# Pacing two gathers per pair of tiles, and moving early row additions, in a mixture-of-experts and attention kernel

## The reference

```python
x = x + 0.5 * ffn(layernorm(x))
x = x + attention(layernorm(x))
x = x + 0.5 * ffn(layernorm(x))      # the same weights

def ffn(x):                                  # 2048 tokens
    scores = softmax(x @ gate.T)             # 32 experts in 8 groups, the best 3 groups count
    weight, index = top_k(masked scores, 6)  # weights are normalised to sum 1
    y = sum over experts e of combine[:, e] * ((silu(x @ w1[e].T) * (x @ w3[e].T)) @ w2[e].T)
    shared = (silu(x @ sw1.T) * (x @ sw3.T)) @ sw2.T
    return y + shared

def attention(x):                            # 16 heads of 16, linear attention with decay
    q, k, v = silu(x @ Wq), silu(x @ Wk), x @ Wv, q and k rotated by position
    o = causal sum with decay in chunks of 128 tokens, with a carried state
    o = rmsnorm per head of o * sigmoid(x @ Wg1 @ Wg2), times a weight
    return o @ Wo
```

## Time and profile before

| | us |
|---|---|
| median of 3 runs | 966.11 (962.2 to 973.23) |
| profiled execution | 960.5 |
| its span | 958.7 |
| PE busy | 772.8 |
| DVE busy | 513.0 |
| POOL busy | 465.3 |
| ACT busy | 358.5 |

### The profile page before, as it was taken

One profiled execution on the slowest core, in us unless ns is written; L12 is line 12 of the kernel. 1 busy time (PEld: TensorE's weight loads), 2 busy tenths in 40 slices (PEclk: granted clock), 3 DMA queues, 4 the chain that ended last, 5 costly groups with the idle time before them and its releaser, 6 DMA issues. The chain is left out here.

```text
span 958.7 us, 16120 instructions
## 1 busy us (share of the span) xinstructions
PE 772.8 (81%) x4554; PEld 609.0 (64%) x4555; DVE 513.0 (54%) x1439; ACT 358.5 (37%) x799; POOL 465.3 (49%) x487
## 2 busy tenths in 40 slices
PE   6895997999969789788889575686999995867486
PEld 6464885888847546576677374564888884645154
DVE  5774942434313537888887469672444431135274
ACT  3160443444424314465665224233444442322000
POOL 3005665553053335867754320655555406456884
PEclk9979898999988898999999755688999998887798
DMA  6862465643233463222220140233444413334524
GB/s 209 338 286 77 158 214 176 231 164 120 89 121 114 159 227 89 80 76 67 72 62 2 34 176 1 77 121 120 153 158 154 138 77 121 126 112 131 207 82 153
DMA packets 42358, 126.43 MB, mean 132 GB/s; under 512 B 8352, under 2 KB 16704, under 8 KB 39488
## 3 DMA queue, kind: packets, MB, share of 16 engines
q1 hardware_dynamic: 23872, 75.40, 20.7%
q0 software_dynamic: 18432, 50.36, 18.0%
HBM read 76.44 MB, written 49.28 MB: 131 GB/s over the span
## 5 line engine op out<-in xcount | busy, mean ns | idle before, releaser
L399 POOL DMA_INDIRECT back<-token_table,slots x192 | 186.7, 973 | 221.9 <-DVE slots L644 96.3
L911 PE MATMUL bank<-w,xt 128*128 x1024 | 260.7, 400 | 33.2 <-ACT xt L492 18.4
L911 PEld LDWEIGHTS bank<-w,xt 128*128 128x128 f32 x1024 | 196.5, 200 | 69.4 <-issue 44.2
L420 POOL DMA_INDIRECT back<-slot_table,combine x124 | 130.0, 1049 | 143.6 <-SPq L328 42.2
L690 DVE TENSOR_TENSOR mids<-mids,bank 128x256 f32<-128x256 f32 x128 | 53.8, 420 | 256.6 <-ACT mids L469 197.3
L931 PE MATMUL bank<-w,mids 128*128 x512 | 142.9, 405 | 4.5 <-DVE mids L697 2.6
L492 ACT COPY xt<-ring 128x256 f32 x256 | 91.5, 408 | 104.0 <-issue 75.9
L931 PEld LDWEIGHTS bank<-w,mids 128*128 128x128 f32 x512 | 93.2, 203 | 16.0 <-issue 7.1
L469 ACT ACTIVATE mids<-bank 128x256 f32<-128x256 f32 x128 | 49.0, 383 | 145.2 <-PE bank L911 87.8
L680 DVE COPY ring<-bank 128x512 f32 (+1 forms) x96 | 66.1, 689 | 46.6 <-PE bank L901 31.2
L923 PE MATMUL bank<-const,mids 128*128 128x128 f32 x256 | 52.6, 290 | 45.7 <-DVE mids L690 24.2
(11 more groups left out here) (209 smaller groups left out, 1070.9 us busy)
## 6 DMA issues: line engine op xcount, KB each, us to landing
slot_table<-gT SPq DMA_DIRECT2D x32, 512.0 KB
slot_table<-ey SPq DMA_DIRECT2D x32, 512.0 KB
w<-in_w SPq DMA_DIRECT2D x12, 1024.0 KB, 17.1
slot_table<-w SPq DMA_DIRECT2D x6, 1024.0 KB
token_table<-back SPq DMA_DIRECT2D x8, 512.0 KB, 2.9
back<-token_table,slots POOLq DMA_INDIRECT x192
x<-in_x SPq DMA_DIRECT2D x4, 512.0 KB, 5.7
turn_a<-in_turn SPq DMA_DIRECT2D x4, 512.0 KB
```

Of the source, the lines that this page charges most:

```text
L399: pool.indirect_dma_start(out=rows[q % RX][:, a * H:(a + 1) * H], out_offset=None, in_=table, in_offset=bass.IndirectOffsetOnAxis(ap=slots ...
L420: pool.indirect_dma_start(out=returned[g % len(returned)], out_offset=None, in_=y_table, in_offset=bass.IndirectOffsetOnAxis(ap=combine[:, ...
L911: last = nc.tensor.matmul(bH[u % 2][:, a * 2 * I:(a + 1) * 2 * I], xt[u % 2][:, a * H + k * P:a * H + (k + 1) * P], w13[:, bass.ds(expert[ ...
```

## The change

It has four parts. (1) Table gathers keep a lead of 4 pairs throughout, in both blocks, and row gathers are let go two per pair from pair 48 (first block) or 47 (second block) on. (2) Rows that come back get more buffers: the space of the first 6 experts in w13 and w2, 18 row buffers, used once these experts' pairs are done; the weights are loaded again at the end of attention. The first column of the first block is added after the last pair, the second in attention as a fifth row; the first two columns of the second block are added after the last pair. (3) In the second block the shared expert's tokens are loaded back in four pieces ahead of SP's last four stores, into free space of the ring. (4) `s_again` becomes four semaphores.

```diff
+GONE = 6
+ADDS = REST + EARLY - 1
+PACED = NQ - NT, NQ - NT - 1
@@
+        spared = [part[:, i * H:(i + 1) * H] for part, n in ((w13, GONE * WE // H), (w2, GONE)) for i in range(n)]
+        s_early = [sem(f"s_early{n}") for n in range(EARLY)]
@@ (first block, then second)
-                    returned = [part[:, i * H:(i + 1) * H] for part, n in ((back, NT), (s1, KS * TB // H))
-                                for i in range(n)]
+                    returned = [back[:, i * H:(i + 1) * H] for i in range(NT)] + spared
...
-                    s1, gTs = w13[:, 0:KS * TB], [w13[:, (u + 1) * KS * TB:(u + 2) * KS * TB] for u in range(2)]
-                    again = w13[:, 3 * KS * TB:3 * KS * TB + KC * T]
-                    returned = [back[:, i * H:(i + 1) * H] for i in range(KEEP)]
+                    products = GONE * WE
+                    s1, *gTs = [w13[:, products + n * KS * TB:products + (n + 1) * KS * TB] for n in range(3)]
+                    spare = (NB % RR + 1) * P
+                    again = [ring[:, a:a + KC * TB] for a in (spare, spare + KC * TB, SPAN + spare, 0)]
+                    returned = [back[:, i * H:(i + 1) * H] for i in range(KEEP)] + spared
@@ (SP)
-                        turns = NQ // 2 // RY - (f == 0)
+                        turns = NQ // 2 // RY - 2
...
+                        sp.wait_ge(e_h, done + NQ - EDGE)
                         if f == 0:
-                            sp.wait_ge(e_h, NQ - EDGE)
                             sp.dma_start(area[:, 0:KC * len(LATE) * TB], columns_table[:, 0:KC * len(LATE) * TB]
                                          ).then_inc(s_here, 16)
+                        else:
+                            stored = columns_table.rearrange("p (k i t) -> p i k t", k=KC, t=TB)
+                            for it in range(T // TB):
+                                sp.dma_start(again[it].rearrange("p (k t) -> p k t", k=KC), stored[:, it]).then_inc(s_again[it], 16)
+                        for it in range(turns, turns + 2):
                             for u in range(RY):
-                                store(turns, u)
+                                store(it, u)
...
                         if f == 1:
-                            sp.wait_ge(e_h, done + NQ)
-                            sp.dma_start(again, columns_table).then_inc(s_again, 16)
@@ (POOL)
-                            if f == 0 and AHEAD <= q < EDGE + RX + AHEAD:
-                                pool.wait_ge(e_xp, q - AHEAD - max(0, q - EDGE - AHEAD) // EDGE + 1)
-                            elif AHEAD <= q < EDGE + AHEAD:
+                            if q >= AHEAD:
                                 pool.wait_ge(e_xp, read + q - AHEAD + 1)
-                            elif q >= RX:
-                                pool.wait_ge(e_xp, read + q - RX + 1)
...
+                                if g == (KEEP if f else NT):
+                                    pool.wait_ge(e_h, done + GONE * NT // 2)
+                                    pool.wait_ge(e_yp, done + GONE * NT // 2)
                                 if g >= len(returned):
                                     pool.wait_ge(s_add, g - len(returned) + 1)
-                                if f == 0 and g % 2 == 0:
-                                    pool.wait_ge(e_h, NQ - NT - 3 + g // 2)
+                                if g % 2 == 0 and PACED[f] + g // 2 <= NQ:
+                                    pool.wait_ge(e_h, done + PACED[f] + g // 2)
@@ (DVE)
-                                if final:
-                                    for g in range(i * 2 * NT // n, (i + 1) * 2 * NT // n):
-                                        add_row(g // NT, g % NT)
...
-                        with dve.Fori(0, (NQ - EDGE - NP) // 2) as it:
+                        with dve.Fori(0, (NQ - NP) // 2 - 1) as it:
                             pairs(it * 2 + NP, 2)
-                        pairs(NQ - EDGE, EDGE, final=True)
+                        pairs(NQ - 2, 2)
                         copy_mid(NQ - 1, NQ - 1)
-                        if f == 1:
...
+                        if f == 0:
+                            for i in range(NT):
+                                add_row(0, i, 0, 2 * len(its))
+                        else:
...
-                            add_rows(2)
+                            add_rows(0, 0)
                             product(0)
-                            add_rows(3)
+                            add_rows(1, 0)
                             product(1)
...
@@ (attention: SP, POOL, DVE)
+                        sp.wait_ge(add_ok, NT * ADDS)
+                        sp.dma_start(w13[:, 0:GONE * WE], w13_in[:, 0:GONE * WE]).then_inc(s_big, 16)
+                        sp.dma_start(w2[:, 0:GONE * H], w2_in[:, 0:GONE * H]).then_inc(s_big, 16)
...
-                                    dve.wait_ge(back_ok[j % RB], (j // RB + 1) * REST * 16)
+                                    dve.wait_ge(s_early[1], NT * 16)
...
+                                if k == 1:
+                                    dve.wait_ge(back_ok[j % RB], (j // RB + 1) * REST * 16)
+                                row = back[j % RB][:, (k - 1) * H:k * H] if k else spared[i]
+                                col = i * TOPK + (k - 1 if k else REST)
```

More of the change, by code:

```diff
@@ L272, in moe @@
                 columns = TOPK if f else EARLY
-                s_back = [sem(f"s_back{k}") for k in range(columns)]
+                s_back = [sem(f"s_back{k}") for k in range(columns)] if f else s_early
                 s_last = [sem(f"s_last{q}") for q in range(4)] if f else []
@@ L1600, in _ @@
                         shifted_mean(3, 1)
-                        for k in range(1, REST):
+                        for k in range(1, ADDS):
                             add_rows(k)(4, 0)
```

77 lines of the change are left out of this document (39 added, 38 removed).

## The result

The changed kernel takes 911.26 us as the median of four runs (907.91 to 912.49), against 964.91 us for the kernel before beside it: a ratio of 0.942, 95% interval 0.936 to 0.949. That is faster, and by more than was forecast. Of the kernel before, the ratios here take only the runs within 1.5% of its fastest, while the medians take all of them. The profiled execution takes 907.91 us, with a span of 906.1 us where the earlier trace rows has 958.7.

A forecast was written before the change was run, and what follows sets the result against it. The expert pair loop was taken as the bound, with ACT stopped by POOL's gapless gather trains. From a 958.7 us span, 61.4 gained and 2, 4 and 23.2 lost gave 926.5, hence 931 us as median; range 911 to 957.

The forecast's parts named there:

- (a): Token gathers, first block, pairs 12 to 16: lead of 4 pairs instead of 8, 23.15 us against 13.67, gain 9.5 us.
- (g): Tail after the last silu: 62 gathers remain, some lengthened by DVE's addition trains; 100.1 us against 76.9, loss 23.2 us.
- Rival 1: ACT's stops are code loads, not gather trains; gains lost and costs stay, 990 us; chance 12%.
- Rival 2: Trains stop ACT, but stores, shared tokens or late column releases still hold it; half the gain, 959 to 962 us; 12%.
- rival 3: Tail: gathers cannot run beside DVE's additions, five trains cost 32 us instead of 15.4; 948 us median; chance 10%.
- (c): Result-row gathers, first block, pairs 48 to 63, two per pair: 17.3 us available, gain taken as 14.3 us.
- (d): Result-row gathers, second block, pairs 48 to 63: 35.2 us available, 6 off for a store behind shared tokens, gain 29.2.
- control of 47.81 us: Undisturbed time assumed for pairs 48 to 63 in both blocks: 3 x 13.31 + 7.88 us.
- (e): Entry into attention: DVE does 16 additions after the last copy instead of 4; cost 2 us, bounds 0 and 4.8.
- (f): Inside attention: DVE gets 16 more additions, which POOL's gathers meet; cost 4 us, bounds 0 and 7.7.
- (b): Token gathers, second block, pairs 1 to 8: lead of 4 pairs, 35.61 us against 27.23, gain 8.4 us.
- 2.7 us added for the median: Half the 0.6% by which the runs' median exceeds the profiled run, added to 928.3 us to give 931 us.

The follow-up runs named there:

- second pair of profiles: Kernel before and changed kernel, both unchanged, profiled again on one chip with stops: 963.59 us and 911.84 us, ratio 0.946.
- the first kernel of set 1: Changed kernel with the table gathers' old lead of up to 8 pairs put back: 934.65 us, ratio 0.963 to the kernel before.
- the second 4.4 us before its end: Changed kernel with row gathers no longer let go two per pair: 980.31 us, ratio 1.009 to the kernel before.
- set 4: Later set with stops, changed kernel run unchanged beside the kernel before (span 961.8 us): 911.84 us, ratio 0.946.
- set 5: Set without stops, changed kernel run unchanged beside the kernel before (884.3 us): 887.33 us, ratio 1.003.

## Why the prediction was right, and where it was wrong

Right: the direction, where the stops are, and what removes them. The stops were at the trains and went with them, and undoing either pace brought them back in its own stretch alone. (a) forecast 9.5 us and measured 9.5. (g) forecast 23.2 and measured 24.4, with its count of 62 gathers, and long gathers only near the end of DVE's trains; that it came so near is in part luck, since the last gather starts 1.4 us earlier than forecast (91.1 and not 92.5; four of the five trains have a long gather) and what follows it takes 2.6 us more (10.2 and not 7.6). Its "56 of 96 gathers behind it" is a misreading, 52 at the last silu in the trace, but the sum doesn't use it. Rival 1 (code loads) is refuted: the same code stops or doesn't with the pace of POOL, the changed kernel's code stops at its start with stops and not without, and nine of the ten waits in the kernel before have no code packet in them. Rival 2 (half of the gain) and rival 3 (a gather can't run beside additions at all, 32 us) didn't come.

Wrong was the size, 926.5 us of span forecast and 906.1 measured, and the steps that failed are those in which I left something over without a row for it:

- (c) and (d): "I take 14.3: some stop at the entry to new code is likely to remain" and "I take 6 us off". Measured 18.8 (17.3 were there to be had) and 36.6 (35.2): nothing remained, on the first profile and on the second. The control of 47.81 us for 15 pairs was itself above what they take undisturbed, 46.3 and 46.5. The reservation in (d), a store held behind the tokens, was an argument without a row, and the kernel that loads the tokens late shows it empty (46.3 against 46.5). These two are 11.9 us of the 20.4.
- (e) and (f): 2 and 4 us were booked, the whole stage grew by 0.7 (on the second pair of profiles it shrank by 0.3). DVE's idle time before the barrier took all 12 additions; the bound of 0 that the earlier trace rows gave was the right end. In attention ten steps take 103.5 us and not 102.7.
- (b): forecast 8.4, measured 10.4 and, the second time, 9.2. The control that I used, pairs 1 to 8 of the first block at 27.2 us, has a piece of a stop in it itself: without stops it is 25.8.
- A further 2.8 us came at pair 1 of the second block (9.0 to 6.1). They can't be booked to the change: on the second pair of profiles it is 9.0 and 9.3, with the stop of 8.3 us still there.

The 2.7 us added for the median were needed (the median lies 3.4 above the profiled run). In the second pair of profiles (d) and (g) come out as 42.7 and 30.7, and together they are the same, 12.0 us of gain against 12.2. One half of this can be followed: the kernel before loses 5.9 us more in its last pairs there and 3.4 less in its tail, with 40 gathers left and not 44. The changed kernel's tail is 2.9 us longer, with five long gathers and not four; why is open.

What the prediction could not see is that the stops come and go with the set. With them the change is worth 50 to 54 us, without them it costs 1 to 4 us (ratio 1.002 to 1.005). That the result was measured with stops, like the profile before it, is luck: in a set without, the same forecast would have been wrong by its whole gain. The tail's 24 us don't show as a loss there. So the kernel before either has a longer tail without stops or loses time elsewhere; it was not profiled in such a set, and this stays open.

## What to carry to other kernels

Where an engine's wait has a releaser that the trace doesn't know, lay the timeline of the engine that issues indirect gathers beside it: if the wait ends inside or some 2 us after a gapless train of them, put a wait or a small operation between the gathers before looking at bytes or code. Size such a gain by the undisturbed stretch alone, without a reserve that no row supports. And measure on more than one chip and at more than one time: here one and the same change is worth 5 to 6% in two comparisons and nothing in a third.

## What the runs showed of the hardware that was not expected

**A train of gathers delays the other engines.** With stops, an issue every 1.25 us without a gap (0.95 us plus 0.30) can keep ACT, DVE and POOL standing for 5 to 17 us in the pairs though what they wait for is done: in the first kernel of set 1 ACT goes on 1.8 us after the train, in the second 4.4 us before its end. A gap of 0.9 us between gathers (1.9 us apart) is enough for no stop at all in the pairs. An eighth of the bytes changes nothing. It is not all: the train of 62 gathers in the changed kernel's tail stops nobody, the train of 44 in the kernel that loads its tokens late holds ACT for 27.2 us. Ten steps of attention, where POOL issues trains of four, take 103.5 us in the changed kernel with stops and 96.4 without, so these trains probably cost something too. What makes the difference, and which piece of hardware or of its software delays the engines, is not known.

**The same kernel is with stops in one set and without in another.** The changed kernel takes 911.8 us in set 4 and 887.3 in set 5. Whether the chip, its machine or the time decides was not tried. Between the two kinds of sets the trace differs in one more thing, which a reader can use to tell them apart. The page's list of DMA issues, the stores of the pairs, in the changed kernel's profile with stops and then without:

```profile
slot_table<-gT SPq DMA_DIRECT2D x32, 512.0 KB
```

```profile
slot_table<-gT SPq DMA_DIRECT2D x32, 512.0 KB, 2.7
```

With stops the page has no time to landing for these stores and the table gathers, in all 14 profiles; without stops it has, in all six. So the signals that show as "remote" are probably those whose records are missing. The instruction traffic is the same in both (29 packets of 0.48 MB and 25 or 26 of 0.20 MB), so the Trainium skill, "Runtime: NRT & Kernel Launch", section on instruction fetch mechanics, by which a taken branch out of the loaded pages stalls, doesn't explain the difference.

**What a train of additions does to a gather.** DVE's train of 850.89 ends at 857.31, and the long gather of 854.89 at 858.14; the train of 877.82 ends at 881.86, the gather of 877.85 at 882.69; before, the one of the earlier trace rows ends at 892.67, the gather of 888.27 at 893.51. Each time the gather ends 0.83 or 0.84 us after the train, while the two ahead of it take 1.1 to 1.3 us. So it is held to the train's end, as the Trainium skill, "SBUF — State Buffer", section on who interferes with whom, has it for two SBUF inputs. The trace agrees on that gather and not on the ones before it: two pass beside the train before one is caught, and beside the 16 additions from 817.31 to 823.73 four pass, with 0.95 to 1.28 us, and none is caught.
